# Last attention of an audio tower on one core: turning lag three, third probability buffer, causal mask added by DVE

## What is computed

```python
def _L3_attn_ref(x, Wq, Wk, Wv, Wo):            # H = 8 heads of width 128
    q = proj(Wq) / scale; kk_ = proj(Wk) / scale; v = proj(Wv)
    dot = jnp.einsum('bhtd,bhsd->bhts', q, kk_)
    dot = jnp.where(causal[None, None], dot, -jnp.inf)
    attn = jax.nn.softmax(dot, axis=-1)
    out = jnp.einsum('bhts,bhsd->bhtd', attn, v)
    return out.transpose(0, 2, 1, 3).reshape(b, t, h * k) @ Wo.T
```

## Time and profile before

| | us |
|---|---|
| median of three runs | 4616.09 |
| the profiled execution | 4617.71 |
| its span in the trace | 4615.9 |
| PE busy | 4177.5 (91%) |
| DVE busy | 2783.5 (60%) |
| ACT busy | 2903.9 (63%) |
| last attention alone (batch 3) | 4388.5 to 4548.3 |

### The profile page before, as it was taken

How to read it: one execution, slowest core, us unless ns; L and a number is a source line. 1 busy time by engine, 2 the same in 40 slices (tenths; PEclk the granted TensorE clock), 3 DMA queues, 4 the chain that set the end, 5 groups by cost and what they waited for, 6 DMA issues and landing times.

```text
span 4615.9 us, 66988 instructions
## 1 busy us (share of the span) xinstructions
PE 4177.5 (91%) x24723; PEld 2308.0 (50%) x24723; DVE 2783.5 (60%) x6451; ACT 2903.9 (63%) x6181; POOL 693.1 (15%) x466
## 2 busy tenths in 40 slices
PE   6788679999999999999999999868889888988988
PEld 4455434444444444444444444335556555555565
DVE  5655567777777777777777777522452344344244
ACT  1222247777777787777777777674665574474533
POOL 0000112222222222222222222100000000000000
PEclk9868779999999999999999999989999999999999
DMA  2000043324242424334242424000000000000000
GB/s 108 1 28 0 23 47 48 51 41 63 38 65 39 53 45 50 59 43 57 39 60 49 53 39 51 24 31 28 32 1 23 21 1 14 27 1 5 23 4 4
DMA packets 94421, 160.48 MB, mean 35 GB/s; under 512 B 18272, under 2 KB 75024, under 8 KB 93712
## 3 DMA queue, kind: packets, MB, share of 16 engines
q1 hardware_dynamic: 94096, 156.20, 20.3%
HBM read 74.04 MB, written 7.82 MB: 18 GB/s over the span
## 4 chain that ended last, share of the span: by engine, by line
PE 76%; DVE 9%; ACT 6%; issue 6%; DVEq 2%; POOL 1%; DMA 1%; POOLq 0%; PEld 0%; PEldq 0%; SPq 0%; ACTq 0%
PE ps L1131 12%; PE ps L1167 12%; PE ps L1487 11%; PE ps L1141 10%; PE ps L1201 4%; PE ps L1210 3%; PE ps L1122 2%; PE ps L1543 2%; PE ps L1018 2%; PE ps L1419 2%; PE ps L1579 2%; DVE peaks L2180 2%; PE ps L1230 2%; PE ps L1003 1%; PE ps L1031 1%
## 5 line engine op out<-in xcount | busy, mean ns | idle before, releaser
L2180 DVE TENSOR_REDUCE peaks<-ps 128x1 f32<-128x748 f32 (+1 forms) x1536 | 1408.9, 934 | 480.8 <-PE ps L1141 458.4
L1750 ACT ACTIVATE masked<-ps 128x384 f32<-128x384 f32 (+3 forms) x1536 | 683.5, 486 | 193.8 <-PE ps L1131 181.6
L1750 ACT ACTIVATE probs<-ps 128x384 f32<-128x384 f32 (+1 forms) x1536 | 663.2, 484 | 73.8 <-PE ps L1131 73.4
L892 POOL TENSOR_TENSOR rstd<-var,minus_half 128x6 f32<-128x6 f32 x104 | 138.3, 1329 | 2899.9 <-DVE var L2413 1510.2
L1131 PE MATMUL ps<-shared 98*128 98x384 bf16 (+3 forms) x1536 | 447.2, 327 | 4.4 <-ACT probs L1750 1.7
L1131 PE MATMUL ps<-q_stack,k_stack 98*128 98x384 bf16 (+3 forms) x1536 | 449.7, 328 | 1.0
L1141 PE MATMUL ps<-k_stack,q_stack 96*128 96x374 bf16 (+1 forms) x1536 | 380.5, 329 | 36.1 <-DMA k_stack<-parts 21.9
L1141 PE MATMUL ps<-shared 96*128 96x374 bf16 (+1 forms) x1536 | 372.2, 323 | 7.4 <-DVE peaks L2180 6.5
L1131 PEld LDWEIGHTS ps<-shared 98*128 98x128 bf16 (+1 forms) x1536 | 148.0, 103 | 336.4 <-ACT masked L1750 125.9
L1131 PEld LDWEIGHTS ps<-q_stack,k_stack 98*128 98x128 bf16 (+1 forms) x1536 | 149.6, 103 | 328.4 <-ACT masked L1750 121.2
L1141 PEld LDWEIGHTS ps<-k_stack,q_stack 96*128 96x128 bf16 (+1 forms) x1536 | 154.6, 105 | 158.5 <-DVE peaks L2180 43.1
(11 more groups left out here) (550 smaller groups left out, 7670.8 us busy)
## 6 DMA issues: line engine op xcount, KB each, us to landing
shared<-parts SPq DMA_DIRECT2D x192, 187.0 KB, 9.2
wr<-in_l SPq DMA_DIRECT2D x32, 580.5 KB, 3.6
q_stack<-parts SPq DMA_DIRECT2D x96, 187.0 KB, 8.0
k_stack<-parts SPq DMA_DIRECT2D x96, 187.0 KB, 10.0
wts<-in_l SPq DMA_DIRECT2D x32, 514.5 KB, 3.5
wrow<-in_l_rows SPq DMA_DIRECT2D x32, 320.0 KB, 4.2
wq<-in_l SPq DMA_DIRECT2D x32, 192.0 KB, 3.4
const<-in_const SPq DMA_DIRECT2D x1, 4202.5 KB, 12.3
```

Of the source, the lines that this page charges most:

```text
L892: pool.tensor_tensor(lane.rstd, lane.var, minus_half[:, :], ALU.pow).then_inc(S["rstd_ready"], 1)
L1750: act.activation(probs_ring(u)[0:m, 0:hi - lo], src[0:m, 0:hi - lo], ACT.Exp, scale=float(HD) ** -0.5).then_inc(S["ring_done"], 1)
L2180: v.tensor_reduce(peaks[0:m, g, j, head:head + 1], src[0:m, :, 0:T // 2], XY, ALU.max)\
```

## The change

Entries are turned three steps behind their scores and weighed four behind, instead of two and three. PE's order in a step becomes: first half turned, weighing, second half turned, fill. DVE copies the turned half first in its step, then divides. A third probs buffer and a second probsT, shared by the lanes, lie in the room behind the last experts' weights. PE's mask product is gone; DVE adds the mask to the diagonal tile in PSUM, drains, and takes the maximum after it.

```diff
@@ -398,6 +398,10 @@
+SPREAD_LAG, WEIGH_LAG = 3, 4
 def slot_of(entry):
@@ -412,7 +416,7 @@
 def last_attention_cost(i):
-    tiles = [last_entry(i - lag)[2] for lag in (0, 2, 3)]
+    tiles = [last_entry(i - lag)[2] for lag in (0, SPREAD_LAG, WEIGH_LAG)]
     fill, spread, weigh = (0 if u is None else u + 1 for u in tiles)
@@ -442,7 +446,7 @@
     if part == 2:
-        return [(("last", i), last_attention_cost(i)) for i in range(len(LAST) + 3)]
+        return [(("last", i), last_attention_cost(i)) for i in range(len(LAST) + WEIGH_LAG)]
     steps = norm_steps("h") + [(("logits",), 1.2)]
@@ -566,7 +570,7 @@
         k_stack0 = sb("k_stack", [P, E, TP], BF16)
-        maskb = sb("maskb", [P, 3 * P], BF16)
+        maskb = sb("maskb", [P, 2 * P], BF16)
         identb = sb("identb", [P, P], BF16)
@@ -720,6 +724,17 @@
         HEADS_BANK, SPREAD_BANK = 3, 4
+        SPARE = E * W4_END + P - E * W4_END % P
+        more_probsT = tokens(shared[:, SPARE:SPARE + TP])
+        more_probs = shared[:, SPARE + TP:SPARE + 2 * TP]
+        def last_probs(lane, i):
+            return (*lane.probs, more_probs)[LAST_UNIT[i] % 3]
+        def last_probsT(lane, i):
+            return (lane.probsT, more_probsT)[LAST_UNIT[i] % 2]
@@ -1530,35 +1545,37 @@
-                    what, e, u = last_entry(i - 3)
+                    at = i - SPREAD_LAG
+                    turned_tiles = last_entry(at)[2] + 1 if last_entry(at)[0] == "score" else 0
+                    def spread(half):
+                        for j in range(3 * half, min(3 * half + 3, turned_tiles)):
+                            mm = pe.transpose(ps[:, SPREAD_BANK, (j % 3) * P:(j % 3 + 1) * P],
+                                              last_probs(lane, at)[:, j * P:(j + 1) * P], ident)
+                        mm.then_inc(S[f"spread{half}_{k}"], 1)
+                    what, e, u = last_entry(i - WEIGH_LAG)
+                    if what == "score" and u < 3:
+                        taken(k)
+                    elif what == "score":
+                        pe.wait_ge(S[f"taken1_{k}"], n.take(f"taken1_{k}"))
+                    if turned_tiles:
+                        slot_done(at)
+                        spread(0)
                     if what == "score":
                         tiles = u + 1
-                        if LAST_UNIT[i - 3]:
+                        if LAST_UNIT[i - WEIGH_LAG]:
                             pe.wait_ge(S[f"heads_done_{k}"], n.take(f"heads_done_{k}"))
                         slot_done(LAST_AT["value", e, None])
+                        for j in range(tiles):
+                            mm = pe.matmul(ps[:, HEADS_BANK, 0:D], last_probsT(lane, i - WEIGH_LAG)[:, j, :],
+                                           lane.V[e % 2][:, j, :], start=(j == 0), stop=(j == tiles - 1))
+                        mm.then_inc(S[f"heads_ready_{k}"], 1)
+                    if turned_tiles > 3:
                         taken(k)
-                        if tiles > 3:
-                            pe.wait_ge(S[f"taken1_{k}"], n.take(f"taken1_{k}"))
-                        for j in range(tiles):
-                            mm = pe.matmul(ps[:, HEADS_BANK, 0:D], lane.probsT[:, j, :], lane.V[e % 2][:, j, :],
-                                           start=(j == 0), stop=(j == tiles - 1))
-                        mm.then_inc(S[f"heads_ready_{k}"], 1)
-                    def spread(half):
-                        what, e, u = last_entry(i - 2)
-                        if what != "score" or u < 3 * half:
-                            return
-                        if half == 0:
-                            slot_done(i - 2)
-                        else:
-                            pe.wait_ge(S[f"taken0_{k}"], n.now(f"taken0_{k}") + 1)
-                        for j in range(3 * half, min(3 * half + 3, u + 1)):
-                            mm = pe.transpose(ps[:, SPREAD_BANK, (j % 3) * P:(j % 3 + 1) * P],
-                                              lane.probs[LAST_UNIT[i - 2] % 2][:, j * P:(j + 1) * P], ident)
-                        mm.then_inc(S[f"spread{half}_{k}"], 1)
-                    spread(0)
+                        spread(1)
                     what, e, u = entry = last_entry(i)
@@ -1576,18 +1593,12 @@
                         for a in range(keys // width):
-                            pe.matmul(ps[:, first + a, 0:width], tile_of(lane.QT[e % 2], u),
-                                      lane.xT[:, a * width:(a + 1) * width], start=True, stop=False,
-                                      skip_group_check=True)
-                        left = diagonal_left(keys, u)
-                        lo, hi = keys - left - (keys // width - 1) * width, width
-                        mm = pe.matmul(ps[:, first + keys // width - 1, lo:hi], identb[:, :], maskb[:, 2 * P:2 * P + left],
-                                       start=False, stop=True, skip_group_check=True)
+                            mm = pe.matmul(ps[:, first + a, 0:width], tile_of(lane.QT[e % 2], u),
+                                           lane.xT[:, a * width:(a + 1) * width], start=True, stop=True)
                     if what is not None:
...
                         n.take(f"slot_done_{k}")
-                    spread(1)
-                    if i == len(LAST) + 2:
+                    if i == len(LAST) + WEIGH_LAG - 1:
                         n.take(f"heads_done_{k}")
@@ -1947,10 +1958,10 @@
                 def last(lane, k, i):
-                    what, e, u = last_entry(i - 2)
+                    what, e, u = last_entry(i - SPREAD_LAG)
                     if what == "score" and u >= 3:
                         act.wait_ge(S[f"spread1_{k}"], n.take(f"spread1_{k}"))
-                        act.activation(flat(lane.probsT[:, 3:u + 1, :]), ps[:, SPREAD_BANK, 0:(u - 2) * P], ACT.Copy)\
+                        act.activation(flat(last_probsT(lane, i - SPREAD_LAG)[:, 3:u + 1, :]), ps[:, SPREAD_BANK, 0:(u - 2) * P], ACT.Copy)\
                             .then_inc(S[f"taken1_{k}"], 1)
@@ -1961,7 +1972,7 @@
                         act.wait_ge(S[f"max_ready_{k}"], n.take(f"max_ready_{k}"))
-                        act.activation(cut(lane.probs[at][:, 0:keys], keys), slot_ap(entry, keys), ACT.Exp,
+                        act.activation(cut(last_probs(lane, i)[:, 0:keys], keys), slot_ap(entry, keys), ACT.Exp,
                                        bias=lane.neg_top[:, at:at + 1], scale=float(D) ** -0.5,
@@ -2261,7 +2272,6 @@
             v.tensor_copy(maskb[:, 0:2 * P], C("band"))
-            v.tensor_copy(maskb[:, 2 * P:3 * P], C("causal")[:, (NT - 1) * P:NT * P])
             v.tensor_scalar(add_w[:, 32:40], C("onehot8"), C("w2_2"), None, ALU.mult)
@@ -2539,32 +2549,38 @@
                 def last(lane, k, i):
-                    what, e, u = last_entry(i - 3)
+                    what, e, u = last_entry(i - SPREAD_LAG)
                     if what == "score":
-                        unit = LAST_UNIT[i - 3]
+                        tiles = min(3, u + 1)
+                        v.wait_ge(S[f"spread0_{k}"], n.take(f"spread0_{k}"))
+                        v.tensor_copy(flat(last_probsT(lane, i - SPREAD_LAG)[:, 0:tiles, :]),
+                                      ps[:, SPREAD_BANK, 0:tiles * P]).then_inc(S[f"taken0_{k}"], 1)
+                    what, e, u = last_entry(i - WEIGH_LAG)
+                    if what == "score":
+                        unit = LAST_UNIT[i - WEIGH_LAG]
                         rtotal = lane.rtotal[:, unit % 2:unit % 2 + 1]
...
                                                ALU.mult, ALU.add).then_inc(S[f"heads_done_{k}"], 1)
-                    what, e, u = last_entry(i - 2)
-                    if what == "score":
-                        tiles = min(3, u + 1)
-                        v.wait_ge(S[f"spread0_{k}"], n.take(f"spread0_{k}"))
-                        v.tensor_copy(flat(lane.probsT[:, 0:tiles, :]), ps[:, SPREAD_BANK, 0:tiles * P])\
-                            .then_inc(S[f"taken0_{k}"], 1)
                     what, e, u = entry = last_entry(i)
...
                         v.wait_ge(S[f"slot_ready_{k}"], n.now(f"slot_ready_{k}"))
+                        last_part = slot_ap(entry, keys) if keys <= 512 else slot_ap(entry, keys)[:, 1, :]
+                        left, width = diagonal_left(keys, u), keys if keys <= 512 else keys // 2
+                        v.tensor_tensor(last_part[:, width - left:width], last_part[:, width - left:width],
+                                        C("causal")[:, (NT - 1) * P:(NT - 1) * P + left], ALU.add)
+                        v.drain()
                         v.tensor_reduce(lane.top[:, at:at + 1], slot_ap(entry, keys), XY if keys > 512 else X, ALU.max)
...
                                         ALU.mult).then_inc(S[f"max_ready_{k}"], 1)
-                    if i == len(LAST) + 2:
+                    if i == len(LAST) + WEIGH_LAG - 1:
                         v.drain()
```

## The result

The changed kernel takes 4638.99 us (median of five runs, 4636.07 to 4640.26) against 4616.09: 1.0047 times as long, 95% interval 1.0035 to 1.0059. It is slower by 23 us. The forecast was 4606, the range reached to 4632. The profiled execution took 4638.99 us, its span is 4637.2, which is 21.3 more than the span before.

A forecast was written before the change was run, and what follows sets the result against it. The prediction took PE, busy 91% of the span, as the bound: its own work and its waits. A gain of 2.5 us in the lone stage plus 7.7 in three woven ones, rounded to 10, gave 4606 us; range 4584 to 4632.

The forecast's parts named there:

- keep 2.6 us for a stage, 7.7 us for three: Three woven stages: the removed product's gain stays whole, new waits being paid by a better order; 7.7 us less.
- PE's product, 10.2 us off: Last attention: removing 192 mask products saves PE a slot of 0.053 us each, 10.2 us of work.
- costs only where PE stands behind it: DVE's add in PSUM: 0.28 us plus 0.08 us drain, 69 us of DVE work, costing only where PE waits.
- replay: One expert stepped through in the stage running alone: period 18.42 us for 18.74, waits even at 3.90, stage gains 2.5.
- the turning's wait for a late exponential: Woven stages: PE's 5.3 us wait at the turning for an exponential late on ACT was to stay.
- Rival A: Woven stages: PE waits for DVE, 22 us more, lone stage 2.5 less; 4635 in full, 4626 by half; chance 0.22.
- The rival's threshold: DVE's add and drain past 0.44 us, where the lone stage's period is back at 18.74 us, make slower decide.
- Rival B: Woven stages: the shifted order removes 6 us of late waits on ACT each; 28 us less, 4588; chance 0.20.
- the 5 us that I had set as the sign of being wrong about the lags: Lone stage: PE's idle time, expected still near 26 us, falling by more than 5 us would refute the lags' part.
- plus 0.62 us: Lone stage, DVE: each maximum takes its reduction (0.94 us for 748 columns, 0.28 for 128) plus 0.62 us.
- Each 0.1 us is 0.4 us an expert: Lone stage: four maxima stand in series, so each 0.1 us of add cost lengthens an expert by 0.4 us.
- Rival C: Woven stages: deeper lags free nothing, waits grow 0.3 us an expert; only the lone stage's 2.5 stay, 4613; chance 0.18.

The follow-up runs named there:

- The corners: Eight kernels: PE's mask product or DVE's add, old or new lags, old or new order of woven steps; 4597.7 to 4658.3 us.
- The experiments on spare SBUF: Kernel with new lags and PE's product, plus an unread DVE add in SBUF: ahead of the reduction 4648.4 us, behind the maximum 4627.3 us.
- The kernel with the add behind the maximum: Kernel with new lags and PE's product, plus an unread DVE add in spare SBUF behind the scaled maximum: 4627.3 us.

## Why the prediction was wrong

**The sign was wrong, and the step that failed is the woven one, "keep 2.6 us for a stage, 7.7 us for three".** It took the product's slots as won and DVE's add as covered. The three stages gave 28.3 us more (11.6 + 9.8 + 6.9), because the add stands in the chain that PE waits for: the mask's move costs 32 to 41 us, whatever the lags and the order.

1. *PE's product, 10.2 us off.* The spacing was read rightly, but I counted it as if PE never stood still behind it. In the kernel before the product is worth nothing (4620.1 against 4618.4), and with the new lags 3.3 us. What PE saves it then waits: in the lone stage of the kernel before without its mask PE is busy for 2.1 us less (131.5 for 133.6) and idle for 1.3 more (27.5 for 26.2). My own rule, that a term counts only where no other work covers it, I applied to DVE's add and not to this.

2. *DVE's add, "costs only where PE stands behind it".* The price was right (0.297 us for 0.28). The share that reaches the end was not: I let the added 0.31 us cost something only in the lone stage, by replay, and counted no wait for it in the woven stages except at the fill of tile 4. The corners show 32 to 41 us for 192 adds, 0.17 to 0.21 us for each, net of PE's product. The argument "DVE is under half busy" was the wrong one, since a share of busy time says nothing about a chain: PE gives scores, DVE finds the maximum, ACT takes the exponential, PE turns it, DVE copies, PE weighs, and two score banks tie the start of this chain to its middle. The add stands in it, and again in DVE's queue ahead of the copies of other entries. The experiments on spare SBUF put the two parts at some 21 and 29 us. I also kept the turning's wait for a late exponential in the woven stages; the lags alone cut it from 4.7 to 0.9 us in the second one.

3. *Rival A was the mechanism, and its size was near.* It asked 9.9 us of DVE's delay for a woven stage. The kernel after against the same kernel with PE's product shows 10.7, 13.2 and 7.0. Its full price was 4635; measured 4639. That the two totals are so near is partly luck: it had 22 us more in the woven stages and 2.5 less in the lone one, and they gave 28.3 more and 8.2 less. I gave it 0.22 and let the range end at 4632, short of its own full price. Its place was named too narrowly, though: the adding attention's weighing (L1448 in the kernel after), which it made 4.3 us, has 1.6 of the 9.6 us of idle time that the add brings to the second woven stage, the last attention's waits for DVE's copy 3.8, and the rest is spread.

4. *The rival's threshold was wrong.* I wrote that it decides from 0.44 us for add and drain. They took 0.37, and it decided. The threshold came from the lone stage's replay, which has nothing to say about the stages where the cost fell.

5. *Rival B's mechanism was there too.* I gave the order 0.4 us for an expert; alone it is worth 20 us, of which the stages and stretches place 17. The stretches between the stages, 2 to 3 us each, I had not looked at; with the new lags they are back at 144 us, so the lags undo that part. In the kernel after the order's gain is real (19 us against the old order) and is spent on the add.

6. *The lone stage: right sign, too small.* It gained 8.2 us where I forecast 2.5. PE's idle time there fell from 26.2 us to 20.6, by 5.6: past the 5 us that I had set as the sign of being wrong about the lags. The waits of PE in the lone stage of the kernel after:

```profile
PE ps L1553 <- DVE parts L2556: 8.6, 9, 1.7
PE ps L1596 <- ACT parts L1975: 6.1, 8, 1.2
PE ps L1553 <- ACT parts L1964: 2.9, 8, 0.4
```

The replay had named all three. It gave 1.07 us an expert to the turning behind DVE's copy (measured 8.6 / 8 = 1.08), 0.87 to the fill that waits for the exponential (6.1 / 8 = 0.76), and 0.88 to ACT's copy of second halves (2.9 / 8 = 0.36); the last fell from 13.6 us in the kernel before to 2.9. The two waits of a weighing for DVE's copy, 0.53 and 0.55 us an expert, did not come: the whole stage shows 0.5 us. The period is the distance between the query products of two experts, on PE:

```profile
4473.22 1.42 PE L1585 MATMUL ps<-k_stack,shared 128*128 128x384 f32 x4
...
4490.69 1.42 PE L1585 MATMUL ps<-k_stack,shared 128*128 128x384 f32 x4
```

It is 17.47 us, against 18.42 by the replay and 18.74 before. By the replay's own slots (14.52) the waits are then 2.95 us, where it had 3.90. Eight times 1.27 is 10.2; 2.0 of it are lost at the ends of the stage, where the deeper pipe has a step more (argued, not measured). The sub-step that was mis-sized is "plus 0.62 us" around each reduction, and the gap I laid behind DVE's operations. The timeline inside that expert:

```profile
4483.18 0.15 DVE L2581 TENSOR_SCALAR wrow<-wrow 128x1 f32<-128x1 f32 x1
...
4483.25 0.15 DVE L2562 RECIPROCAL wrow<-wrow 128x1 f32<-128x1 f32 x1
...
4483.48 0.35 DVE L2565 SCALAR_TENSOR_TENSOR k_stack<-ps,wrow,k_stack 128x128 f32<-128x128 f32 x1
4483.75 0.29 DVE L2576 TENSOR_TENSOR ps<-ps,const 128x128 f32<-128x128 f32 x1
4484.11 0.69 DVE L2579 TENSOR_REDUCE wrow<-ps 128x1 f32<-128x512 f32 x1
```

The scaling ends at 4483.33 by its duration and the next operation is there at 4483.25, 0.08 us earlier; the add at 4483.75 starts 0.08 us before the division's end at 4483.83. I had counted some 0.07 us after such operations instead. That is 0.15 us at each such step of a chain with four maxima in series; that these steps make up the whole 0.95 us is an estimate, no run shows it.

7. *What the replay said of the add in the lone stage looks right, in part by luck.* "Each 0.1 us is 0.4 us an expert": 0.31 us makes 1.24, less the product's 0.32, times eight, 7.4 us. The lone stage shows 7.2 (151.6 against 144.4). But apart, the add is 8.1 there (151.6 against 143.5 with no mask) for 9.9, and the product 0.9 (144.4 against 143.5) for 2.6; the two misses cancel. Without the add the lags gain 15.4 us there.

8. Outside the last attention nothing moved, as said. Rival C, in which the waits eat the product's 0.32 and no more, gave 4613 and did not hold.

What stays open: why the new lags cost 6 to 8 us in a woven stage in the old order and 1 to 4 in the new one, and why they take back the order's gain in the stretches between. The runs show that they do, not which of the 111 moved steps matters; I did not try single steps. Nor does any run separate the waits of a stage from the clock that falls with them; how far the clock alone can go, the last section shows.

## What to carry to other kernels

Moving work from the busiest engine to a half-idle one was paid for by the chain here, not by the busy share: ask whether the receiving engine's operation stands between two turns of the busy one, and count it there in full before counting what the busy engine saves, which may only turn into waiting. Price a removed term as carefully as an added one, by leaving it out alone if you can. Where a merged order depends on cost constants, the reordering is a change of its own (some 20 us here), so run it apart from the edit that caused it, and keep each part of a change in the stages where it pays.

## What the runs showed of the hardware that I had not expected

**PE's clock pays for waits.** A woven stage at a granted clock of 0.96 has PE idle 33.6 us (the kernel before in the new order), at 0.93 it is 46.3 us (the kernel after), at 0.90 it is 49.7 us (the kernel after in the old order); PE's busy time rises with it from 200.3 to 201.8 to 205.6 although the latter two have some 50 products fewer. Inside the first woven stage of the kernel after one such wait can be read, on PE:

```profile
3387.46 0.40 PE L1553 MATMUL ps<-const,probs 128*128 128x128 f32 x1 [3.42 <-ACT probsT L1964]
...
3387.65 2.36 PE L1572 MATMUL ps<-V,probsT 128*128 128x128 f32 x10
...
3389.81 2.08 PE L1589 MATMUL ps<-shared,xnT 128*128 128x128 f32 x12
```

and the same two operations later in that stage, without a wait ahead of them:

```profile
3452.57 1.29 PE L1572 MATMUL ps<-V,probsT 128*128 128x128 f32 x10
3453.69 1.50 PE L1589 MATMUL ps<-shared,xnT 128*128 128x128 f32 x12
```

After 3.42 us of idle PE the ten products take 2.16 us from start to start (3387.65 to 3389.81) for 1.12 (3452.57 to 3453.69), close to twice as long: the lower of the clock's two levels, 1.2 for 2.4 GHz. The granted clock of the two stretches behind the wait is 0.54 and 0.71; it was 1.00 during the wait and is 1.00 again after them:

```profile
3384.00:3387.40 3.40, 0.04 (x1) 0.00 (x0) 0.88 (x3) 3.40 (x7) 0.00 (x0) 1.00 0.00 0
3387.40:3389.80 2.40, 2.34 (x11) 2.34 (x12) 0.36 (x2) 0.46 (x3) 0.00 (x0) 0.54 0.01 3
3389.80:3391.90 2.10, 2.10 (x15) 2.10 (x14) 0.35 (x1) 0.00 (x0) 0.00 (x0) 0.71 0.00 0
3391.90:3394.00 2.10, 2.10 (x15) 1.07 (x18) 0.49 (x2) 2.08 (x3) 0.00 (x0) 1.00 0.00 0
```

This wait cost itself and, by these clocks, some 1.7 us more behind it (2.40 x 0.46 and 2.10 x 0.29, an estimate). The mean granted clock of the 20 us from 3380 to 3400 is 0.91, for 1.00 in the same window of the kernel before.

The idle time alone does not set the clock. The kernel with the add behind the maximum has nearly the same waits in its first two woven stages, and PE idle for 42.1 and 43.4 us of them, but its granted clock is 0.93 in the first and 0.96 in the second, which is 5.4 us shorter:

```profile
3247.20:3492.00 244.80, 202.74 (x1359) 138.85 (x1360) 124.37 (x406) 142.92 (x264) 2.64 (x2) 0.93 0.04 14
3635.80:3875.20 239.40, 196.04 (x1359) 133.32 (x1360) 124.58 (x408) 142.69 (x264) 2.65 (x2) 0.96 0.03 9
```

So some 5 us of a stage can lie in the clock and not in the change; which waits bring it down, no run here shows.

**DVE's small operations overlap.** With nothing to wait for, the next one starts 0.07 to 0.08 us before the end of the last (timeline above). An add and its drain take 0.36 to 0.38 us from start to the next start, 0.07 over the add's duration: a drain between the two takes the overlap away and adds nearly as much.
